# Making layer 1's coefficients in one run ahead of the second aggregation instead of between its steps

## The chip, the cores and the metric

The kernel runs on one core of a Trainium2 chip. What counts is the device time of one execution, in microseconds. Three runs are shown for the kernel before; the time is their median. The profiled execution is a separate one.

## What is computed

Four graph layers follow one another on 1250 nodes with 512 features and 21250 edges, sorted by their target node. The part that matters here is layer 0, which is two relational convolutions, and the coefficients of layer 1:

```python
def _rel_graph_conv(h, src, dst, etypes, norm, basis, comp, bias, loop_w, apply_relu):
    hb = jnp.einsum('nd,bdo->bno', h, basis)
    coef = comp[etypes]
    m = coef[:, 0, None] * hb[0][src]
    for b in range(1, basis.shape[0]):
        m = m + coef[:, b, None] * hb[b][src]
    m = m * norm[:, None]
    agg = jax.ops.segment_sum(m, dst, num_segments=n)
    out = agg + bias + h @ loop_w
...
# layer 1: 32 relations, 8 bases
weight = jnp.einsum('rb,bio->rio', w_comp, bases)
h_rel = jnp.einsum('ni,rio->rno', x, weight)
msg = h_rel[etype, src] * norm
out = jax.ops.segment_sum(msg, dst, num_segments=n_nodes)
```

Layer 0 is called twice with its own weights; its relu'd first result is `h` of the second. Each layer's result is added to its input and normalized.

## The kernel before

**Order of the work.** The program is laid out by hand: each stage writes its instructions for all five engines, and each engine runs its own list in that order, held back by semaphores. The stages are: `prepare` (tables of the sorted edges and the coefficients of layer 0), the first aggregation L0a, the first transform (with `Hidden` as its epilogue), the second aggregation L0b, the second transform, the aggregation L1 of layer 1, its transform, and then layers 2 and 3.

**An aggregation** (`aggregate`, L769) multiplies gathered rows by selectors. GpSimd gathers 168 tiles of 128 edges' source rows by indirect DMA (L809) into a ring of 16 places (`gathered`); SyncE counts their landings (L838). For each of 208 steps VectorE makes a 128 x 128 selector (L945) out of the edge's place in its window and its coefficient, and TensorE multiplies the selector by the tile (L895), in two passes since both are fp32. ScalarE copies a finished window's sum out (L922) and clears the bank (L913, L927). Banks 0 to 3 of PSUM take the sums. Near the end, and after it, TensorE turns the sums (L858) for the transform. VectorE may be 12 selectors ahead. TensorE and VectorE read small tables of step numbers into registers every four steps (L812).

**The coefficients** (`Coefficients`, L603) are the entries of `comp` by the edge's relation, times the edge's weight. For layer 1 there are 62 groups of 4 steps, in 16 batches of 4 groups (the last has 2). A batch k is made in three moves, and every fourth time a fourth:
- `spread(k)` (L684): TensorE spreads the relations of the steps over the partitions, 4 matmuls of 128 columns in 16 bits, stationary tile `step_pickers`, into bank 4. Layer 1 has this one bank for spreads, so `spread(k)` waits for `compare(k - 1)`.
- `compare(k)` (L693): VectorE compares the bank with the relation's number, 512 elements, into `relation_onehot`.
- `pick(k)` (L703): TensorE picks the rows of `comp_blocks`, 4 fp32 matmuls of 32 columns in two passes each, into bank 5 or 6.
- `weigh(k)` (L722): VectorE multiplies 16 groups by the edges' weights into `coef_L1`. There are 4 of these.

Layer 0's coefficients are made in `prepare`, by `on_pe` and `on_dve` of the same class in a row, in 4 batches, with two banks for spreads and 128 columns per pick. Layer 1's are made inside L0b: `beside_on_pe(s)` and `beside_on_dve(s)` put a spread, a compare, a pick and a weighing after every ninth step. The pickers, a copy of 4096 16-bit elements per partition (L661), are laid by ScalarE at L0b's head (`work.lay(act.copy, laid)`).

**Beside the steps of L0b** also runs `OwnProduct`: 10 tiles of h times the loop weight, 4 slices each, two passes a slice (L1027), each slice after a step.

**The head of L0b.** `ready` is what every engine waits for before it begins: the first transform's last products, the turned tiles of h in `xT` (`hidden.done()`, copies L1232 and L1251) and the stores of h to `hidden_rows` in DRAM (L1196, five of them last). The gathers read `hidden_rows`; nothing else in the aggregation does.

Of the kernel before, what the change touches and what calls it, by code (L numbers as in the profile page):

```python
# [13 lines left out]
P = 128  # L14
# [3 lines left out]
D = 512  # L18
# [145 lines left out]
def prepare(C):  # L164
# [355 lines left out]
        engine.wait_ge(*numbered.now())  # L520
    dve.wait_ge(*taken.now())
    dve.wait_ge(*of0.weighed.now())
    C.tables_made = [taken.now(), of0.weighed.now(), keyed.now()]


# [240 lines left out]
SUM_BANKS = 4  # L766


def aggregate(C, name, path, nb, rows, G, ready, counting=None, beside=()):  # L769

# [7 lines left out]
    space, steps, windows, co = M.at, path.steps, path.windows, C.coef[name]  # L780
    xs = M.new("gathered", [P, RING, D])
    sel = M.new("selector", [P, SELECTORS, P])
    grid = C.iota[:, 0:path.nodes]
    gathered = [C.landed(f"gathered{u}") for u in range(LANDINGS)]
    tiles_landed, multiplied = C.event(f"tiles_landed_{name}"), C.event(f"multiplied_{name}")
# [33 lines left out]
    def on_pool():  # L819
        if counting:  # L820
            for t in range(RING):
                gather(t)
        for token in ready:
            pool.wait_ge(*token)
        if not counting:
            for t in range(RING):
                gather(t)
        for first in range(RING, T, BATCH):
            over = [v & COUNTED for v in table(C.steps_of_tile[path][0:1, first - RING:first - RING + BATCH], POOL, 1, steps)]
            for t in range(first, first + BATCH):  # L830
                pool.wait_ge(multiplied.semaphore.sem, over[t - first])
                pool.sem_inc(*place_free.inc())
                gather(t)
# [50 lines left out]

    def on_pe():
        for token in ready:
            pe.wait_ge(*token)
        tiles, rows_of, sums, counts = batch(0)
        for s in range(steps):
            pe.wait_ge(*selected(s + 1))  # L890
            if counting:
                pe.matmul(counts[s % BATCH], counting.rows[:, s % SELECTORS, :], counting.sources[:, s % SELECTORS, :],  # L892
                          start=False, stop=False, skip_group_check=True)
            pe.wait_ge(tiles_landed.semaphore.sem, tiles[s % BATCH])
            pe.matmul(sums[s % BATCH], sel[:, s % SELECTORS, :], rows_of[s % BATCH], start=False, stop=False,  # L895
                      skip_group_check=True).then_inc(*multiplied.inc())
            if (s + 1) % BATCH == 0 and s + 1 < steps:
                tiles, rows_of, sums, counts = batch((s + 1) // BATCH)
            if turns_after(s) is not None:
                turn(turns_after(s))  # L900
            for work in beside:
                work.beside_on_pe(s)
        for j in late:
            turn(j)
# [45 lines left out]
    def on_dve():  # L950
        for token in ready:
            dve.wait_ge(*token)
        if counting:
            dve.wait_ge(*counting.numbered(1))
        for s in range(steps + AHEAD):
            if s < steps:
                if s % BATCH == 0:
                    begun = [v & COUNTED for v in table(C.window_of_step[path][0:1, s:s + BATCH], DVE, 1, windows)]
                select(s, begun[s % BATCH])
            if s >= AHEAD:  # L960
                for work in beside:
                    work.beside_on_dve(s - AHEAD)
                if turns_after(s - AHEAD) is not None:
                    for k in range(KC):
                        take(turns_after(s - AHEAD) * KC + k, dve)
        for j in late:
            for n in range(j * KC, (j + 1) * KC):
                if taker[n] is dve:
                    take(n, dve)
# [92 lines left out]
def plain_lhs(xT):  # L1062
    return lambda k, js: xT[:, k, js[0] * P:(js[0] + len(js)) * P].rearrange("p (j n) -> p j n", n=P)
# [455 lines left out]
def layers_0_1(C):  # L1519

    nc, A, M = C.nc, C.A, C.M
    pe, act, dve, pool, sp = C.engines
    hidden_rows, x1_rows = C.rows("hidden_rows"), C.rows("x1_rows")
    C.x1_rows = x1_rows
    C.count_rows = nc.dram_tensor("count_rows", (NP, NP), F32, kind="Internal").ap()

    G, after_G, counting = C.G0, C.after_G, C.counting
    tail = (M.end - 4 * (2 * NT * D + 2 * D)) // 64 * 64
    M.at = after_G
    turned = aggregate(C, "L0a", PATH0, 4, A["x"], G, C.tables_made, counting)  # L1530

    M.at = tail
    x = M.new("x", [P, NT, D])
    xT = M.new("xT", [P, KC, NP])
    assert M.at <= M.end
    M.at = tail - 4 * HALF * D
    h = M.new("h", [P, HALF, D])
    M.at = after_G
    products = [(basis_lhs(4, G, b), A["L0_gnn_basis0"][b]) for b in range(4)]
    hidden = Hidden(C, h, xT, hidden_rows)  # L1540
    turn_x = TransposeX(C, x, xT, 4 * KC)
    multiplied = transform(C, products + [(plain_lhs(xT), A["L0_gnn_loop0"])], A["L0_gnn_bias0"], turned, [], hidden, turn_x)
    assert M.at <= tail
    M.at = after_G
    ready = multiplied + hidden.done() + [stored.now() for stored in hidden.stored]
    own = OwnProduct(C, tail, x, xT, A["L0_gnn_loop1"], A["L0_gnn_bias1"], ready)
    turned = aggregate(C, "L0b", PATH0, 4, hidden_rows, G, ready, beside=(C.of_layer1, own))

    products = [(basis_lhs(4, G, b), A["L0_gnn_basis1"][b]) for b in range(4)]
    residual = ResidualNorm(C, lambda j: x[:, j, :], x1_rows)  # L1550
    multiplied = transform(C, products, None, turned, [own.added.now()], residual)

    M.at = C.after_layer1_edges
    G = M.new("G1", [P, PATH1.windows, D])
    keep1 = M.at
    ready = multiplied + [residual.ln.normed.now()] + [s.now() for s in residual.stored]
    turned = aggregate(C, "L1", PATH1, 8, x1_rows, G, ready)

    M.at = C.after_small
    C.x_place = M.at  # L1560
    C.x = x = M.new("x_L2", [P, NT, D])
    C.condT, C.condR = M.new_split("condT", [STACKED, NP])
    C.count = M.new("count_by_src", [P, NT, NP])
    C.keep2 = M.at
    C.rows_place = (M.end - 64 - 4 * (2 * N + 2 * NT * 4 * P)) // 64 * 64
    condition = Conditioning(C)
    assert M.at <= C.keep2
    M.at = C.keep2
    C.W2 = M.new("weights2", [P, 2, KC, D])
    assert M.at <= C.after_layer1_edges + 4 * D * PATH1.windows // 2  # L1570
    M.at = keep1
    C.layer1_norm = residual = ResidualNorm(C, lambda j: x[:, j, :], None, x1_rows)
    products = [(basis_lhs(8, G, b), A["L1_gnn_bases"][b]) for b in range(8)]
    C.layer1_done = transform(C, products, A["L1_gnn_h_bias"], turned, [], residual, other=condition)
    C.conditioned = condition.chain.now()
# [1274 lines left out]
```

## Time and profile before

| | us |
|---|---|
| three runs | 3026.91, 3029.58, 3031.84 |
| median | 3029.58 |
| profiled execution, its own time | 3030.57 |
| profiled execution, its span | 3029.2 |

| engine | busy us | share of the span |
|---|---|---|
| TensorE | 2912.4 | 96% |
| VectorE | 1783.0 | 59% |
| ScalarE | 1201.4 | 40% |
| GpSimd | 1117.0 | 37% |

The span is what the trace covers; 1.4 us of the execution's time lie around it. A time inside the span is told from the span's start. L0b begins near 435 and ends near 694. In the views PE is TensorE, PEld its loading of stationary tiles, DVE is VectorE, ACT is ScalarE, POOL is GpSimd, and SP is SyncE with the queue SPq. An engine's busy time is a sum over its instructions; a matmul's end is modelled, so pieces of one engine may overlap. PEclk is the granted clock of TensorE as a share of 2.4 GHz, so that 0.50 is 1.2 GHz.

### The profile page before, as it was taken

What the parts mean: (1) busy time and instruction counts of PE and PEld (TensorE: products, weight loads), DVE (VectorE), ACT (ScalarE), POOL (GpSimd) and SP (SyncE); (2) the same over time, 40 slices, a digit from 0 to 9 for tenths busy, and PEclk for the clock granted to TensorE, in tenths of its full rate; (3) what the DMA queues carried; (4) which work ended last, traced back from release to release, by engine and by line L of the source; (5) the groups of instructions that cost most, each with busy time, mean ns of one, the idle gap of its engine ahead of it and who ended that gap; (6) DMA issues with size and microseconds to landing.
All of it is one profiled execution on the core that took longest, in us unless ns stands there. A gap on an engine that the chain in (4) does not pass through costs nothing.

```text
span 3029.2 us, 43316 instructions
## 1 busy us (share of the span) xinstructions
PE 2912.4 (96%) x14533; PEld 2175.3 (72%) x14533; DVE 1783.0 (59%) x4790; ACT 1201.4 (40%) x2182; POOL 1117.0 (37%) x930
## 2 busy tenths in 40 slices
PE   6999989999799999999999999999999999999999
PEld 3446764457644568764479988899888998789987
DVE  7774224453433632543667677576775767757677
ACT  1333331113244233421545554355543545435454
POOL 4773337663377533411031134311343113431133
PEclk9999999999899999999999999999999999999999
DMA  4775437652277523232030021300213002130022
GB/s 125 206 206 168 133 105 203 175 171 74 90 206 208 154 77 95 70 110 69 28 115 8 8 70 45 112 8 8 70 45 112 8 8 70 45 112 8 8 70 83
DMA packets 129387, 279.13 MB, mean 92 GB/s; under 512 B 22616, under 2 KB 45464, under 8 KB 128144
## 3 DMA queue, kind: packets, MB, share of 16 engines
q0 software_dynamic: 40320, 132.15, 15.1%
q1 hardware_dynamic: 87408, 141.55, 14.7%
q8 instruction: 123, 2.02, 0.3%
q10 hardware_dynamic: 1440, 2.62, 0.2%
q14 instruction: 96, 0.79, 0.1%
HBM read 227.65 MB, written 27.46 MB: 84 GB/s over the span
## 4 chain that ended last, share of the span: by engine, by line
PE 88%; DVE 8%; ACT 2%; DMA 1%; issue 1%; SPq 0%; POOL 0%; DVEq 0%; ACTq 0%; POOLq 0%
PE banks L895 19%; PE banks L159 17%; PE banks L160 17%; PE banks L161 17%; PE banks L2456 6%; PE banks L2120 3%; PE banks L1769 2%; PE banks L858 2%; PE banks L1027 1%; DMA yT_lo<-yT_new_lo 1%; DVE y_tile L2072 1%; DVE y_tile L2074 1%; PE banks L892 1%; DVE columns L2055 1%; DVE G L869 1%
## 5 line engine op out<-in xcount | busy, mean ns | idle before, releaser
L895 PE MATMUL banks<-gathered,selector 128*128 x1328 | 619.3, 598 | 28.5 <-SPq L838 17.0
L895 PEld LDWEIGHTS banks<-gathered,selector 128*128 128x128 f32 x1328 | 239.2, 192 | 299.2 <-issue 220.7
L2544 ACT CAST probT<-banks 128x512 fp32r<-128x512 f32 (+2 forms) x480 | 212.2, 516 | 263.1 <-PE banks L2456 262.3
L1466 POOL TENSOR_TENSOR weight_parts<-weight_ring,weight_parts 128x512 fp32r<-128x512 f32 x130 | 187.7, 1444 | 300.1 <-ACT weight_parts L1399 300.1
L922 ACT COPY G<-banks 128x512 f32<-128x512 f32 x160 | 93.7, 585 | 509.9 <-PE banks L895 509.9
L2625 DVE CUSTOM_DVE_ANT_0 prob<-banks,count_by_src 128x512 f32<-128x512 f32 (+1 forms) x480 | 258.3, 588 | 59.0 <-PE banks L161 59.0
L2552 DVE TENSOR_TENSOR probT<-banks,probT 128x512 fp32r<-128x512 f32 (+2 forms) x480 | 254.2, 585 | 50.6 <-ACT probT L2544 49.9
L159 PE MATMUL banks<-weight_parts,lhs_parts 128*128 128x512 f32 x680 | 269.1, 396 | 15.0 <-DVE lhs_parts L1410 6.2
L160 PE MATMUL banks<-weight_parts,lhs_parts 128*128 128x512 f32 x680 | 267.4, 393 | 0.0
L161 PE MATMUL banks<-weight_parts,lhs_parts 128*128 128x512 f32 x680 | 267.0, 393 | 0.0
L1425 DVE TENSOR_TENSOR lhs_parts<-G,lhs_parts 128x640 fp32r<-128x640 f32 x122 | 101.4, 833 | 275.7 <-ACT lhs_parts L1397 275.5
L159 PE MATMUL banks<-probT,value_parts_hi 128*128 128x256 f32 (+3 forms) x800 | 234.7, 293 | 0.0
L2578 ACT ACTIVATE prob<-prob,columns 128x1250 f32<-128x1250 f32 x160 | 217.7, 1361 | 41.8 <-DVE columns L2632 41.7
L160 PE MATMUL banks<-probT,value_parts_hi 128*128 128x256 f32 (+3 forms) x800 | 222.2, 278 | 0.0
L161 PE MATMUL banks<-probT,value_parts_lo 128*128 128x256 f32 (+3 forms) x800 | 221.5, 277 | 0.0
L2230 POOL TENSOR_TENSOR lhs_parts<-values_and_heads,lhs_parts 128x512 fp32r<-128x512 f32 x80 | 103.1, 1291 | 312.0 <-ACT lhs_parts L2283 311.7
L2456 PE MATMUL banks<-ident,prob 128*128 128x128 f32 (+1 forms) x1600 | 198.2, 271 | 2.5 <-DVE probT L2552 1.7
L1397 ACT CAST lhs_parts<-G 128x640 fp32r<-128x640 f32 x122 | 88.8, 728 | 271.8 <-PE banks L161 271.2
L809 POOL DMA_INDIRECT gathered<-hidden_rows,src_index x168 | 163.3, 972 | 81.5 <-SPq L838 46.6
L809 POOL DMA_INDIRECT gathered<-x_rows,src_index x168 | 162.9, 970 | 82.1 <-SPq L838 34.4
L809 POOL DMA_INDIRECT gathered<-in_x,src_index x168 | 163.9, 976 | 72.2 <-SPq L838 32.5
L1973 POOL CAST head_weights_hi<-head_weights 128x1024 fp32r<-128x1024 f32 x16 | 16.6, 1039 | 456.6 <-DMA columns<-in_L_gnn_bk 456.6
(300 smaller groups left out, 6814.1 us busy)
## 6 DMA issues: line engine op xcount, KB each, us to landing
weight_ring<-in_L_gnn_basis SPq DMA_DIRECT2D x64, 256.0 KB, 2.7
weight_ring<-in_L_gnn_bases SPq DMA_DIRECT2D x64, 256.0 KB, 2.6
x_L<-x_rows SPq DMA_DIRECT2D x50, 256.0 KB, 4.2
x_rows<-x_L SPq DMA_DIRECT2D x50, 256.0 KB, 5.5
yT_hi<-yT_new_hi SPq DMA_DIRECT2D x4, 2560.0 KB, 10.9
yT_lo<-yT_new_lo SPq DMA_DIRECT2D x4, 2560.0 KB
count_rows<-count SPq DMA_DIRECT2D x10, 640.0 KB, 4.2
count_by_dst<-count_rows SPq DMA_DIRECT2D x10, 640.0 KB, 4.2
```

The lines of the kernel that those rows point to most:

```text
L159: pe.matmul(acc, lhs[0], rhs[0], start=start, stop=False)
L160: pe.matmul(acc, lhs[0], rhs[1], start=False, stop=False)
L161: return pe.matmul(acc, lhs[1], rhs[0], start=False, stop=stop)
L809: pool.indirect_dma_start(xs[:, (t + 1) % RING, :], None, rows, index).then_inc(*gathered[t % LANDINGS].inc())
L895: pe.matmul(sums[s % BATCH], sel[:, s % SELECTORS, :], rows_of[s % BATCH], start=False, stop=False, skip_group_check=True).then_inc(*multi ...
L1466: pool.tensor_tensor(weight_parts[:, n % 2, 1, :], ring[:, n % 4, :], weight_parts[:, n % 2, 0, :].bitcast(F32), ALU.subtract).then_inc(*w ...
L2230: pool.tensor_tensor(lhs_parts[:, j % 2, 1], attnT[:, :, j * P:(j + 1) * P], lhs_parts[:, j % 2, 0].bitcast(F32), ALU.subtract).then_inc(* ...
L2456: ins = pe.transpose(bank[3 + q // 4][0:width, (q % 4) * P:(q % 4) * P + rows], prob[0:rows, t % 2, q * P:q * P + width], C.ident[0:rows, ...
L2544: ins = act.copy(hi, of)
L2552: ins = dve.tensor_tensor(lo, of, hi.bitcast(F32), ALU.subtract)
L2578: act.activation(prob[:, t % 2, :], prob[:, t % 2, :], ACT.Exp, bias=nmax[:, t % 2:t % 2 + 1], scale=scale, accum_out=rsum[:, h % 2, t:t + ...
L2625: dve.tensor_tensor_reduce(out=prob[:, s, c:c + width], in0=bank[n][:, 0:width], in1=count[:, t, c:c + width], scale=1.0, scalar=-2.0 * NE ...
```

## The change

- The coefficients of layer 1 are no longer made beside the steps of L0b. `aggregate` gets an argument `ahead`, and TensorE and VectorE run its whole sequence (`on_pe`, `on_dve`) before their first step.
- VectorE waits for the last weighing before it makes its first selector.
- The head's waits are split: `ready` holds the products and the turned tiles; the stores are `stored`, which GpSimd waits for before its gathers, SyncE before the loads of `OwnProduct`, and TensorE after the coefficients. VectorE and ScalarE no longer wait for the stores.
- The pickers are laid by GpSimd ahead of the first transform, as soon as L0a's last step is over, at an address behind the ring and the selectors that nothing uses until L0b.

```diff
@@ prepare
+    C.kinds_made = taken.now()
@@ aggregate
-def aggregate(C, name, path, nb, rows, G, ready, counting=None, beside=()):
+def aggregate(C, name, path, nb, rows, G, ready, counting=None, beside=(), stored=(), ahead=None):
@@
     sel = M.new("selector", [P, SELECTORS, P])
+    if ahead:
+        assert M.at == ahead.place
+        M.at = ahead.end
@@ on_pool
-        for token in ready:
+        for token in ready + list(stored):
             pool.wait_ge(*token)
@@ on_pe
         for token in ready:
+            pe.wait_ge(*token)
+        if ahead:
+            ahead.on_pe(C.kinds_made)
+        for token in stored:
             pe.wait_ge(*token)
         tiles, rows_of, sums, counts = batch(0)
@@ on_dve
         for token in ready:
             dve.wait_ge(*token)
+        if ahead:
+            ahead.on_dve()
+            dve.wait_ge(*ahead.weighed.now())
@@ layers_0_1
+    coming = C.of_layer1
...
+    M.at = coming.place = after_G + 4 * (RING * D + SELECTORS * P)
+    for token in turned.steps_over:
+        pool.wait_ge(*token)
+    coming.lay(pool.tensor_copy, C.event("pickers_laid"))
+    coming.end = M.at
+    M.at = after_G
     multiplied = transform(C, products + [(plain_lhs(xT), A["L0_gnn_loop0"])], A["L0_gnn_bias0"], turned, [], hidden, turn_x)
-    assert M.at <= tail
+    assert M.at <= coming.place and coming.end <= tail - 4 * HALF * D
     M.at = after_G
-    ready = multiplied + hidden.done() + [stored.now() for stored in hidden.stored]
-    own = OwnProduct(C, tail, x, xT, A["L0_gnn_loop1"], A["L0_gnn_bias1"], ready)
-    turned = aggregate(C, "L0b", PATH0, 4, hidden_rows, G, ready, beside=(C.of_layer1, own))
+    ready = multiplied + hidden.done()
+    stored = [stored.now() for stored in hidden.stored]
+    own = OwnProduct(C, tail, x, xT, A["L0_gnn_loop1"], A["L0_gnn_bias1"], ready + stored)
+    turned = aggregate(C, "L0b", PATH0, 4, hidden_rows, G, ready, beside=(own,), stored=stored, ahead=coming)
```

The class that makes the coefficients is the same in both kernels; these are its parts that the change now calls in a row:

```python
    def on_pe(self, types):
        pe.wait_ge(*types)
        pe.wait_ge(*self.blocked)
        self.spread(0)
        for k in range(len(self.batches)):
            if k + 1 < len(self.batches):
                self.spread(k + 1)
            self.pick(k)

    def on_dve(self):
        for k in range(len(self.batches)):
            self.compare(k)
            if k and self.complete(k - 1) is not None:
                self.weigh(k - 1)
        self.weigh(len(self.batches) - 1)
```

TensorE at the head of L0b, before (L684 is a spread, L895 a step, L812 and L882 the reading of a table; a wait stands in brackets):

```order
L1204 MATMUL banks<-ident_49,h_16350 128x128 x3
L812 TENSOR_LOAD registers_by_step_67 [waits tile1_stored,tile0_stored,tile2_stored,turned_by_dve,tile3_stored,turned_by_act,tile4_stored,half_summed,product]
L882 ISA x4
L894 REGISTER_ALU [waits selected]
L895 MATMUL banks<-gathered_17691,selector_17692 128x512 [waits tiles_landed_L0b]
L684 MATMUL banks<-types_by_step_76,step_pickers_18989 128x128 [waits G_zero_act]
```

TensorE at the same place and at the end of the new run, with the change (L685 is a spread, L704 a pick, L903 a step):

```order
L685 MATMUL banks<-types_by_step_76,step_pickers_16353 128x128 [waits steps_taken,turned_by_dve,relations_numbered,turned_by_act,pickers_laid,half_summed,product]
L685 MATMUL banks<-types_by_step_76,step_pickers_16353 128x128 x3
L685 MATMUL banks<-types_by_step_76,step_pickers_16353 128x128 [waits types_compared]
L685 MATMUL banks<-types_by_step_76,step_pickers_16353 128x128 x3
L704 MATMUL banks<-comp_blocks_87,relation_onehot_80 128x32 [waits types_compared]
...
L704 MATMUL banks<-comp_blocks_87,relation_onehot_80 128x32 [waits types_compared]
L704 MATMUL banks<-comp_blocks_87,relation_onehot_80 128x32
L816 TENSOR_LOAD registers_by_step_67 [waits tile3_stored,tile2_stored,tile4_stored,tile1_stored,tile0_stored]
L886 ISA x4
L902 REGISTER_ALU [waits selected]
L903 MATMUL banks<-gathered_17695,selector_17696 128x512 [waits tiles_landed_L0b]
```

All 16 batches now stand ahead of the first step, and the wait for the stores stands behind them. The same on VectorE, with the change (L694 is a compare, L723 a weighing, L953 a selector):

```order
L1262 COPY xT_16349<-banks 128x4x128 [waits tile_turned] x2
L694 TENSOR_SCALAR relation_onehot_80<-banks,relation_90 128x512 [waits turned_by_dve,turned_by_act,types_spread,half_summed,product]
L694 TENSOR_SCALAR relation_onehot_80<-banks,relation_90 128x512 [waits types_spread]
L694 TENSOR_SCALAR relation_onehot_80<-banks,relation_90 128x512 [waits types_spread,comp_picked] x3
L723 TENSOR_TENSOR coef_L_18_66<-banks,weights_78 128x64x8 [waits comp_picked]
L694 TENSOR_SCALAR relation_onehot_80<-banks,relation_90 128x512 [waits types_spread,comp_picked] x4
...
L694 TENSOR_SCALAR relation_onehot_80<-banks,relation_90 128x256 [waits types_spread,comp_picked]
L723 TENSOR_TENSOR coef_L_18_66<-banks,weights_78 128x56x8 [waits comp_picked]
L816 TENSOR_LOAD window_of_step_58 [waits coefficients]
L952 REGISTER_ALU
L953 SCALAR_TENSOR_TENSOR selector_17696<-iota_60,place_in_window_70,coef_L0b_74 128x128 [waits banks_cleared_L0b]
```

The first selector, which stood right behind the copies of xT and the wait for the stores, now stands behind 16 compares and 4 weighings. On GpSimd the copy of the pickers stands between L0a's last gather and the first transform's first rounding:

```order
L813 DMA gathered_5361<-in_x,src_index_61 128x512 [waits multiplied_L0a,tiles_landed_L0a]
L662 COPY step_pickers_16353<-ident_16bit_79 128x4096 [waits selected,multiplied_L0a]
L1444 CAST weight_parts_16356<-weight_ring_16355 128x512 [waits chunk0_in,selected,multiplied_L0a]
L1446 TENSOR_TENSOR weight_parts_16356<-weight_ring_16355,weight_parts_16356 128x512 [waits G_zero_pool]
```

There it stood in ScalarE's list before, at L0b's head.

## Rows read from the trace of the kernel before

**Rows 1.** The page's part 4, the chain that ended last, by engine.
```profile
PE 88%; DVE 8%; ACT 2%; DMA 1%; issue 1%; SPq 0%; POOL 0%; DVEq 0%; ACTq 0%; POOLq 0%
```

**Rows 2.** Stretches: length, PE busy (instructions), PEclk, DMA share, GB/s.
```profile
20.00:25.00 5.00, 5.00 (x23) 1.00 0.31 84
40.00:45.00 5.00, 5.00 (x16) 0.50 0.53 154
430.00:435.00 5.00, 4.07 (x26) 1.00 0.28 102
435.00:440.00 5.00, 0.00 (x0) 0.69 0.44 166
445.00:450.00 5.00, 3.72 (x8) 0.50 0.90 316
450.00:455.00 5.00, 5.00 (x12) 0.94 0.71 206
```

**Rows 3.** Timeline at L0b's head: start, length, instruction, idle before and releaser.
```profile
434.89 0.58 ACT L1232 COPY xT<-banks 128x512 f32<-128x512 f32 x1 [0.48 <-PE banks L1204]
438.90 3.60 ACT L661 COPY step_pickers<-ident_16bit 128x4096 bf16<-128x4096 bf16 x1 [3.42 <-DMA hidden_rows<-h]
439.58 0.98 POOL L809 DMA_INDIRECT gathered<-hidden_rows,src_index  x1 [13.49 <-DMA hidden_rows<-h]
...
448.15 0.63 PE L684 MATMUL banks<-types_by_step,step_pickers 128*128 128x128 bf16 x4
448.83 0.75 DVE L693 TENSOR_SCALAR relation_onehot<-banks,relation 128x512 f32<-128x512 f32 x1
```

**Rows 4.** Chain of waits in order of time, L0b: start, length, piece.
```profile
446.28 2.08 PE banks L895 x2
448.36 0.42 PE banks L684 x4
448.79 4.43 PE banks L895 x8
...
459.22 1.72 PE banks L895 x4
461.16 3.49 PE banks L895 x8
464.65 0.81 PE banks L703 x8
...
629.00 24.11 PE banks L895 x56
...
691.14 2.58 PE banks L895 x6
```

**Rows 5.** Instructions on the tile `gathered` in 430 to 760: ns min/median/max, first and last start.
```profile
L895 PE MATMUL banks<-gathered,selector x416: 592/592/1222, 446.3 to 693.1; 128*128 x139
```

**Rows 6.** Timeline of `prepare`, layer 0's coefficients among it.
```profile
22.84 0.98 PE L504 MATMUL banks<-tile_of_step_onehot,dst_parts 128*128 128x208 bf16 x4
29.01 2.07 PE L703 MATMUL banks<-comp_blocks,relation_onehot 128*128 128x128 f32 x8 [0.42 <-DVE relation_onehot L693]
41.65 1.12 PE L504 MATMUL banks<-tile_of_step_onehot,dst_parts 128*128 128x248 bf16 x4
46.08 0.26 DVE L943 TENSOR_SCALAR onehot_row<-low_numbers_16bit,row_in_window 128x128 bf16<-128x128 f16 x1 [0.45 <-issue]
```

**Rows 7.** Weighings of layer 1 (line L722): ns min/median/max, first and last start.
```profile
L722 DVE TENSOR_TENSOR coef_L<-banks,weights x4: 982/1103/1106, 499.1 to 629.0; 128x512 f32<-128x512 f32 x3, 128x448 f32<-128x448 f32 x1
```

**Rows 8.** Timeline: GpSimd and TensorE at the first transform's start, GpSimd's last gather of L0b.
```profile
259.51 0.61 POOL L1433 CAST weight_parts<-weight_ring 128x512 fp32r<-128x512 f32 x1 [13.62 <-DMA weight_ring<-in_L_gnn_basis]
262.12 1.28 POOL L1435 TENSOR_TENSOR weight_parts<-weight_ring,weight_parts 128x512 fp32r<-128x512 f32 x1
277.37 0.50 PE L159 MATMUL banks<-weight_parts,lhs_parts 128*128 128x512 f32 x1 [1.93 <-DVE lhs_parts L1410]
...
669.89 0.96 POOL L809 DMA_INDIRECT gathered<-hidden_rows,src_index  x1 [0.30 <-SPq L838]
```

## The prediction

> **What bounds the kernel now.** The chain of waits first: TensorE carries 88% of it, so a change counts where it moves TensorE's own work or lets it stand idle [rows 1]. Then the granted clock around the start of the second aggregation (L0b) [rows 2]: TensorE does nothing in 435 to 440, its clock falls from 1.00 to 0.50 (from 2.4 to 1.2 GHz), and it is back only in the stretch from 450. Then the timeline there [rows 3]: the last tile of xT is copied by 435.47, the stores of the hidden rows let the first gather go at 439.58, and the pickers keep ScalarE busy for 3.60. Last the chain inside L0b [rows 4]: the first step begins at 446.28, when its gathered tile has landed, and from there to 693.7 TensorE waits for nothing. So L0b costs an idle head and then a TensorE-bound stream, and the change moves work from the stream into the head. Does what leaves the stream outweigh by how much the first step comes later?
>
> **What leaves the stream.** Fifteen of the 16 batches of layer 1's coefficients are a spread of four 16-bit matmuls and a pick of eight passes; the last is half a batch. Their cost, read from the stream: from 446.28 to 629.00 are 182.7 us. A pass of a step costs 24.11 / 56 = 0.4305 us. Of the 416 passes of L0b [rows 5] 118 come after 629.00 (56, seven groups of eight, six), so 298 lie before: 128.3 us. The ten own products with 4 slices of 2 passes cost 80 x 0.4305 = 34.4. That leaves 20.0 us. The low clock at the start takes 2.4 of them: 2.08 for two passes where 0.86 is the price, 4.43 for eight where it is 3.44, 0.42 for the first spread where 0.22 is. **17.6 us** are left for the batches, 1.1 each: a pick of 0.81 [rows 4], a spread of 0.22 (460.94 to 461.16), and some 0.1 of change-over [rows 4].
>
> **When the first step now begins.** PE, DVE and ACT no longer wait for the stores, so the first spread can go at 435.6 (435.47 and a semaphore) [rows 3]. Only one bank takes spreads, so spread k+1 waits for compare k, and a batch is bound either by that loop or by TensorE's own work on a spread and a pick.
> - The loop: a spread's results are there for the compare 0.68 after its first matmul (448.15 to 448.83, at 1.2 GHz), the compare takes 0.75 [rows 3], a semaphore 0.05: 1.48.
> - TensorE's work depends on the clock. At 2.4 GHz it is 0.22 + 0.81 = 1.03. At 1.2 GHz the spread is 0.42 [rows 4]; no row shows this pick at 1.2 GHz. From below it is 0.81 (nothing doubles), from above the 2.07 of layer 0's pick, which has the same stationary tiles and four times the columns [rows 6]. I take 1.62, twice the high-clock price, since a pass of a step, too, takes at least twice its 0.43 there (2.08 for two) [rows 4]. A batch is then 2.04, TensorE-bound.
>
> Which clock? Layer 0's coefficients in the first 35 us are the same loop, denser. Their row says 1.00, but the durations are those of 1.2 GHz: four matmuls of 208 columns take 0.98 at 22.84, four of 248 take 1.12 at 41.65, where the row says 0.50, the same rate per column [rows 2, 6]. So that work, on an engine busy 5.00 of 5.00, did not lift the clock. And in L0b the clock is high at 435 and falls soon after the gap begins [rows 2]; the new chain starts 0.7 us into that gap. I take one or two batches at 2.4 GHz and the rest at 1.2.
>
> Sum: 15.5 batches x 2.04 = 31.6, so the picks end at 467.2. Then 0.2 until the last is read, 0.98 for the last weighing [rows 7], 0.45 for DVE's register load (its gap before 46.08) [rows 6], 0.35 for the first selector and 0.05: 469.2. The high-clock batches at the beginning give back 0.9 (1.28 each instead of 2.04, and part of the second): 468.3. The first step moves from 446.28 to 468.3, **+22.0**. The steps start at 1.2 GHz as before, so the 2.4 stay. Sum: +22.0 - 17.6 = **+4.4 us**.
>
> **What costs nothing, and under what cover.** The pickers on GpSimd: 4,096 elements a partition are 4.9 us at the 0.61 of its 512-element cast, and at the 1.28 of its two-input pass 10.2; I take 4.9, the nearer kind. A gain is not possible, as nobody waited there. They start when L0a's last step is done, 256.7, and GpSimd's first rounding moves from 259.51 to 266.9 at worst. Its first two chunks, done at 263.40 before, are then done at 270.8, and TensorE asks for the first at 277.37 [rows 8]. Without DVE's and ACT's turning of G there the 10.2 would show. The three weighings inside the chain (1.10 each [rows 7]) delay a compare by some 0.5, inside the 0.56 by which the loop is shorter than TensorE's batch; at 2.4 GHz they show, 0.57 each. ScalarE's 3.60 at 438.90 are freed, but the first step waited for the tile. SP issues what it did, on the same stores. The gathers: the first 16 go as before, from 439.58, fill the ring and wait for the first step; the other 152 cost 1.26 each or less than the stream's pace. Before, the last was issued at 669.89, 21 us ahead of the last steps at 691.14 [rows 4, 8]; that lead is set by the ring and stays, so no step comes to wait for a tile. DVE's compares and weighings leave the steps; TensorE did not wait for them.
>
> The sum against the profiled execution's own 3030.57 is 3035.0; that execution is 1.0 above the median of three, so against 3029.58 it is **3034.0**. A difference under 0.2% (6.1 us) can't be told from none here, and this is 0.15%.
>
> **The rivals.**
> - **The clock stays at 2.4 GHz (15%).** For it: the head's gap is only 0.7 us, and in each batch TensorE is used for 1.03 of 1.28 us. Against: the rows of layer 0. A batch is then the loop, 0.48 + 0.75 + 0.05 = 1.28 (a spread's matmuls 0.20 shorter): 15 are 19.2, the half one 1.3, the delays 1.7, the end 2.0, so the first step is at 459.8, +13.5. The steps start at 2.4 GHz: -2.4. Sum -6.5: 3023.1. The Trainium skill (TensorE: Matmul & The Clock Gate, "HAM oscillation — how this bites in real kernels") warns of gaps between bursts in which TensorE does nothing; read as the only thing that lowers the clock, it would give this rival. The row of 435 to 440 agrees that such a gap lowers it, and layer 0's rows speak against its being the only one [rows 2, 6].
> - **A mixed clock (10%)**, high for half of the batches: 3028 to 3032.
> - **The pick costs layer 0's whole 2.07 (12%)**: at 1.2 GHz its passes are bound by loading 128 x 128 fp32 tiles and don't get under one another, and the next spread waits for their end. A batch is 2.49, 15.5 of them 38.6, the first step at 476.2: +29.9 - 17.6 = +12.3, 3041.9, slower. It decides from a batch of 2.15 us on. For it: a measured row of the same stationary tiles. Against: 0.57 of those 2.07 are the last pass running out, and four times the columns.
> - **The pickers are late or in the way (3%)**: only if the copy took over 16 us; then each us more is one lost at 277.
>
> **How the numbers follow.** The forecast has 60%, its own range 3032 to 3036.5 (batches of 1.95 to 2.15, one to three of them at 2.4 GHz). The range of 8 in 10 reaches from below the high-clock case to the 2.07 case: 3022 to 3042. Faster by over 0.2% is most of the high-clock case: 0.11. Slower by over 0.2% is the 2.07 case, the pickers, and the edge of the forecast's: 0.21. Within: 0.68.
>
> **What would show it.** The first L685 at 435.6 instead of 448.15; sixteen of them 2.0 apart (1.3: first rival; 2.5: third); PEclk 0.50 over most of 437 to 470; the first step near 468; from there to its end a stream of 230, 17.6 shorter, with nothing between steps but own products and turns; GpSimd's copy of 4 to 10 us at 256.7, TensorE's first L159 still near 277. I am wrong in the main point if the clock stays at 1.00 there, or if a batch is not TensorE-bound.

## The result and the profile after

The changed kernel takes 3035.6 us (median of 17 runs, 3029.34 to 3040.04), the kernel before in the same comparison 3029.64 (17 runs). The ratio is 1.0019, with an interval of 1.0012 to 1.0026: 6.0 us longer, inside the 0.2% that was taken as no difference, though above zero. A second comparison of the same two kernels gave 3035.08 against 3030.79, ratio 1.0013 (1.0004 to 1.0022), 4.3 us. The forecast was 3034.0, or +4.4.

The chain of waits of the changed kernel at L0b's head (start, length, piece; lines after 520 have moved, so L685 is the spread, L694 the compare, L704 the pick, L723 the weighing, L903 the step) answers to [rows 3, 4]:

```profile
437.45 0.59 ACT xT L1243
438.05 0.20 issue
438.24 0.40 PE banks L685 x4
438.67 0.05 DVEq L693
438.76 0.76 DVE relation_onehot L694
439.57 0.40 PE banks L685 x4
439.97 0.87 PE banks L704 x8
440.84 0.39 PE banks L685 x4
...
444.04 0.43 PE banks L685 x4
444.47 1.66 PE banks L704 x8
446.12 0.42 PE banks L685 x4
446.55 1.65 PE banks L704 x8
448.20 0.43 PE banks L685 x4
...
467.13 2.52 PE banks L704 x12
469.68 0.99 DVE coef_L L723
470.69 0.34 DVEq L816
471.16 0.36 DVE selector L953
471.52 0.12 issue
471.64 3.78 PE banks L903 x4
```

From the fourth batch on the chain lies on TensorE alone: 0.43 for a spread, 1.65 for a pick, 2.08 from spread to spread. Its end is the short tail of weighing, register load and selector.

The stretches of 5 us (busy time and count of PE, PEld, DVE, ACT and POOL, then PEclk, DMA share, GB/s) give the clock, beside [rows 2]:

```profile
435.00:440.00 5.00, 3.23 (x30) 2.62 (x30) 3.08 (x5) 3.71 (x8) 0.00 (x0) 1.00 0.59 213
440.00:445.00 5.00, 4.95 (x40) 4.75 (x39) 2.67 (x4) 0.34 (x1) 1.96 (x3) 0.76 0.48 164
445.00:450.00 5.00, 5.00 (x30) 5.00 (x30) 2.74 (x4) 0.00 (x0) 3.82 (x4) 0.50 0.98 361
450.00:455.00 5.00, 5.00 (x32) 5.00 (x32) 2.02 (x3) 0.00 (x0) 3.83 (x4) 0.50 0.76 232
```

The clock is at 2.4 GHz for the first batches and then at 1.2 GHz, with TensorE and its loading of stationary tiles (PEld) each busy 5.00 of 5.00.

The instructions on `gathered` in L0b answer to [rows 5], and the timeline of GpSimd at the first transform to [rows 8]:

```profile
L903 PE MATMUL banks<-gathered,selector x416: 592/592/1218, 471.6 to 700.7; 128*128 x139
L813 POOL DMA_INDIRECT gathered<-hidden_rows,src_index x168: 951/957/1102, 442.4 to 678.2; - x168
```
```profile
257.62 3.59 POOL L662 COPY step_pickers<-ident_16bit 128x4096 bf16<-128x4096 bf16 x1 [10.87 <-PE banks L903]
261.17 0.60 POOL L1444 CAST weight_parts<-weight_ring 128x512 fp32r<-128x512 f32 x1
261.85 1.28 POOL L1446 TENSOR_TENSOR weight_parts<-weight_ring,weight_parts 128x512 fp32r<-128x512 f32 x1
```

The pickers put the first rounding back from 259.51 to 261.17, and the last gather is still issued 22 us ahead of the last pass at 700.7 (23 before, 669.89 to 693.1).

**Where the time went.** The two traces don't line up at L0b. The last xT copy starts at 437.45, 2.56 later than before [rows 3], and it can be placed. In L0a TensorE's clock rose a few steps later (0.66 in 50 to 55, before 0.88), so L0a ended 0.9 later; nothing of the change lies there. And in the first transform the clock was down for a few us (0.79 in 280 to 285, before 1.00). Both profiles of the changed kernel have this second fall, but two kernels below that lay the pickers in the same place have not, so it isn't counted as the change's. So everything is measured from that copy, to the start of the last six passes of L0b in the timeline. That timeline ends so in both kernels (before first, then changed):

```profile
690.98 2.74 PE L895 MATMUL banks<-gathered,selector 128*128 x6
```
```profile
698.52 2.74 PE L903 MATMUL banks<-gathered,selector 128*128 x6
```

| kernel (all in the same condition of the chip) | last xT copy | to the first step | first step to last group | both | against before |
|---|---|---|---|---|---|
| before | 434.89 | 11.39 | 244.70 | 256.09 | |
| changed | 437.45 | 34.19 | 226.88 | 261.07 | +4.98 |
| changed, second comparison | 438.40 | 34.40 | 226.66 | 261.06 | +4.97 |
| between the steps, other two parts kept | 435.88 | 11.61 | 244.66 | 256.27 | +0.18 |
| changed, 16-bit picks | 438.88 | 26.26 | 227.45 | 253.71 | -2.38 |
| eight batches ahead, 16-bit picks | 435.10 | 14.07 | 230.56 | 244.63 | -11.46 |

The first step came 22.8 later and the stream was 17.8 shorter: +5.0. The spans differ by 5.1 (3034.3 and 3029.2), because 2.4 of the 2.56 are given back behind L0b. One place shows it: before, TensorE's clock was 0.69 right after L0b, where the changed kernel has 1.00. The stretch from 700 of before and the one from 705 of the changed kernel:

```profile
700.00:705.00 5.00, 5.00 (x17) 3.88 (x17) 1.79 (x2) 0.22 (x1) 1.14 (x1) 0.69 0.29 99
```
```profile
705.00:710.00 5.00, 3.10 (x14) 2.57 (x15) 4.30 (x5) 0.38 (x1) 3.61 (x3) 1.00 0.39 109
```

### The profile page after: what moved, and what is told of

Its sections match the earlier page's. It is cut to its first block, busy times and chain, and to the rows that moved or that the text cites. A ratio compares the mean times of both kernels' runs of the same rounds, so it can differ in the third digit from the quotient of the medians.

```text
span 3034.3 us, 43314 instructions
## 1 busy us (share of the span) xinstructions
PE 2924.8 (96%) x14533; PEld 2188.3 (72%) x14533; DVE 1784.7 (59%) x4790; ACT 1197.8 (39%) x2181; POOL 1121.0 (37%) x931
## 4 chain that ended last, share of the span: by engine, by line
PE 87%; DVE 8%; DMA 2%; ACT 2%; issue 1%; POOL 0%; SPq 0%; DVEq 0%; ACTq 0%; POOLq 0%
PE banks L903 19%; PE banks L159 17%; PE banks L160 16%; PE banks L161 16%; PE banks L2475 6%; PE banks L2139 3%; PE banks L1788 2%; PE banks L862 2%; PE banks L1038 1%; DMA yT_lo<-yT_new_lo 1%; DVE y_tile L2091 1%; DVE y_tile L2093 1%; PE banks L900 1%; DVE columns L2074 1%; PE banks L704 1%; DVE x_L L2306 1%
## 5 line engine op out<-in xcount | busy, mean ns | idle before, releaser
L903 PE MATMUL banks<-gathered,selector 128*128 x1328 | 615.6, 598 | 19.5 <-SPq L842 17.5
L903 PEld LDWEIGHTS banks<-gathered,selector 128*128 128x128 f32 x1328 | 242.1, 192 | 301.8 <-issue 233.2
```

## The experiments

Twelve runs of nine kernels stand below, in three groups. The first and the second ran on one chip, the third on another. In the first and the third the kernel before took 3127.62 and 3128.95 us, against 3030.79 in the second. Each kernel is therefore compared with before in its own group, and traces are compared across groups only for the head and the spacing of batches. The times that were expected in us (3035 to 3036 and the like) were all meant for the condition of 3030.

### First group, with before at 3128: is the batch bound by TensorE, and does filler hold the clock?

**Two banks for the spreads.**
```diff
-    C.of_layer1 = Coefficients(C, PATH1, 32, [(C.coef["L1"], "L1_gnn_w_comp")], (4,), (5, 6), *shared)
+    C.of_layer1 = Coefficients(C, PATH1, 32, [(C.coef["L1"], "L1_gnn_w_comp")], (4, 7), (5, 6), *shared)
```


> The changed kernel with a second bank for layer 1's spreads, so that a spread no longer waits for the compare just before it. Theory (the run ahead is bound by TensorE's own work at 1.2 GHz, 2.08 us a batch): no change, 3035 to 3036, batches still 2.08 apart once the clock is low; only the first three or four batches, at 2.4 GHz, may be 0.2 shorter each. Rival (the loop spread, compare, spread is what bounds a batch): batches fall to 1.1 to 1.5 and the time by 9 to 15 us, to 3021 to 3027.

Measured: 3148.15 against 3127.62, ratio 1.0062 (1.0036 to 1.0087). TensorE's timeline of this kernel:

```profile
481.79 1.03 PE L704 MATMUL banks<-comp_blocks,relation_onehot 128*128 128x32 f32 x8
482.66 0.39 PE L685 MATMUL banks<-types_by_step,step_pickers 128*128 128x128 bf16 x4
482.88 1.07 PE L704 MATMUL banks<-comp_blocks,relation_onehot 128*128 128x32 f32 x8
...
485.71 0.61 PE L685 MATMUL banks<-types_by_step,step_pickers 128*128 128x128 bf16 x4
486.11 1.86 PE L704 MATMUL banks<-comp_blocks,relation_onehot 128*128 128x32 f32 x8
487.79 0.61 PE L685 MATMUL banks<-types_by_step,step_pickers 128*128 128x128 bf16 x4
488.19 1.86 PE L704 MATMUL banks<-comp_blocks,relation_onehot 128*128 128x32 f32 x8
```

At 1.2 GHz batches stay 2.08 apart (485.71 to 487.79); at 2.4 GHz they are 1.09 (481.57 to 482.66) where one bank gave 1.27. So the bank binds only at the high clock, and TensorE binds at the low one. The time can't be set against the changed kernel, which was not run beside it, and the 20.5 us above before have something else in them: VectorE did nothing for 11.89 us in the middle of the run ahead, which no trace of the second group shows. The head is 45.0 (34.2 in the changed kernel), and the stream behind it is longer too, 248.3 (226.9):

```profile
505.66 0.75 DVE L694 TENSOR_SCALAR relation_onehot<-banks,relation 128x512 f32<-128x512 f32 x1 [11.89 <-remote]
```

**One filler matmul, and four, behind each pick.**
```diff
             self.pick(k)
+            if self.relations == 32:
+                for _ in range(1):
+                    pe.matmul(self.C.bank[7][:], self.C.ident16[:],
+                              self.pickers[:, 0:4, :].rearrange("p g r -> p (g r)"), start=True, stop=True)
```
(`range(4)` in the other.) Their results are not used.

> The changed kernel with one more 16-bit matmul of 512 columns behind each pick, whose result nobody reads. Theory (the clock falls because the run uses TensorE too sparsely): if one filler holds the clock at 2.4 GHz, a batch is 1.28 to 1.35, the first step comes 9 to 10 us earlier and starts at full clock, 3023 to 3026. If it doesn't, a batch is 2.08 + 0.43 = 2.5 and the time 3041 to 3043. Rival (the clock in the run costs nothing, a batch is bound by VectorE): 3035 to 3036 either way.

> The same with four fillers behind each pick: TensorE is nearly always streaming. Theory: the clock stays at 2.4 GHz; a batch is 0.22 + 0.81 + 4 x 0.215 = 1.9, so the first step comes at about the changed kernel's own time or 2.5 us earlier, and the steps start at full clock, which saves 2.5 to 3 more: 3030 to 3034. If the clock falls all the same, a batch is 2.08 + 4 x 0.43 = 3.8 and the time 3061 to 3065. The batch length and the granted clock of the run tell it apart.

Measured: 3152.67, ratio 1.0086 (1.0067 to 1.0104), with one; 3162.74, ratio 1.0122 (1.0101 to 1.0143), with four. That is 25 and 35 us above before, where 3023 to 3043 was expected with one, and 3030 to 3034 or 3061 to 3065 with four; and each trace has an idle time of VectorE in the run ahead (10.59 and 13.99), so only the batches are read. With one filler the clock fell after two batches, and the batch was 2.51 (480.24 to 482.75). With four, in this trace, it did not fall:

```profile
480.00:485.00 5.00, 5.00 (x42) 3.58 (x42) 1.65 (x3) 0.00 (x0) 2.92 (x3) 1.00 0.63 190
485.00:490.00 5.00, 4.54 (x40) 3.34 (x38) 2.61 (x3) 0.00 (x0) 3.83 (x4) 1.00 0.98 352
490.00:495.00 5.00, 1.50 (x10) 0.76 (x9) 0.00 (x0) 0.00 (x0) 3.84 (x4) 0.98 0.71 211
```

Batches were 1.95 apart up to an idle time of 13.99 of VectorE at 489.3; after it they ran at 1.2 GHz, 3.79 each, to the end of the run ahead, with TensorE busy 5.00 of 5.00 from 505 to 540. The first half looked like proof that fillers hold the clock. The second half and the repeat below took it back.

**Five batches ahead, eleven between the steps.**
```diff
-    PACE = 9
+    PACE, AHEAD = 9, 5
...
     def beside_on_pe(self, s):
         k, at = divmod(s, self.PACE)
+        k += self.AHEAD
...
-            ahead.on_pe(C.kinds_made)
+            ahead.ahead_on_pe(C.kinds_made)
```


> The changed kernel with only the first five of the 16 batches ahead of the first step, the other eleven after every ninth step as before. Theory (a batch ahead is free as long as it lies in the 10.7 us in which the first gathered tile is still on its way, and costs 2.08 after that, while it saves 1.1 in the stream): five batches end near 445.6 on the clock of before, the first step stays within 1 us of its old place, and 5 x 1.1 = 5.6 us leave the stream: 3024 to 3026. Rival (taking them out of the stream saves less than 0.6 each, or the head is longer for another reason than the batches): 3028 to 3034.

Measured: 3129.4, ratio 1.0002 (0.9988 to 1.0015). The first step came 11.52 after the last xT copy (11.39 before), so the five batches did fit into the head. The gain that should have followed is not in the time.

### Second group, with before at 3031: beside the changed kernel itself

> The changed kernel itself, so that the others of this call have it beside them on their own chip. Both theories: if the chip is like that of the first comparison, +4 to +7 us against the kernel before. On the chip of the first four experiments DVE once had nothing to do for 11 to 14 us inside the run ahead (its releaser is shown as another core or an unknown queue); if that comes with the chip and not with my edits, the changed kernel has such a gap there too and stands +10 to +25 us. If it came with the edits alone, +4 to +7 there as well.

Measured: 3035.08 against 3030.79, ratio 1.0013 (1.0004 to 1.0022). No idle time of VectorE of this kind stands in its trace, on the same chip as the first group. That speaks for a condition of the chip and against the edits as the source of the idle times; the two-bank and filler kernels themselves were not run in this condition. The batches are the same: 0.43 and 1.65.

**Before's order, with the other two parts of the change kept.**
```diff
+    coming.lay(pool.tensor_copy, C.event("pickers_laid"))
...
-    turned = aggregate(C, "L0b", PATH0, 4, hidden_rows, G, ready, beside=(C.of_layer1, own))
+    turned = aggregate(C, "L0b", PATH0, 4, hidden_rows, G, ready, beside=(coming, own), stored=stored, ahead=coming)
```


> Before's order (coefficients between the steps of the second aggregation), with the change's other two parts kept: GpSimd lays the pickers at the first transform, and the first gathers no longer wait for the hidden rows' tables. My theory (both parts are hidden, all of the change's time comes from the order): 0 us against the kernel before, +-2. Rival (the pickers on GpSimd or the split wait cost or save time by themselves): off by 3 us or more, and the first step of the second aggregation not at its place of before.

Measured: 3031.02 against 3030.79, ratio 0.9999 (0.999 to 1.0007). The head is 11.61 and the stream 244.66, within 0.3 of before. TensorE waits for the stores before its first step here, as before, so the split wait is kept for VectorE and ScalarE alone. The pickers on GpSimd and this split are worth nothing by themselves; the change's time is all in the order, which is what uses the earlier start.

**The picks in 16 bits.** The entries of `comp_blocks` are kept as a high and a low 16-bit part, so layer 1's coefficients have another precision; two small VectorE instructions in `prepare` make the parts.
```diff
+                onehot = C.onehot[:, k % 2, :].bitcast(BF16)[:, n * P:(n + 1) * P]
+                for half in range(2):
+                    ins = pe.matmul(to, onehot, self.blocks16[:, half, :], start=half == 0, stop=half == 1)
```


> The change, with layer 1's picks as two bfloat16 matmuls (the coefficients kept as a high and a low 16-bit part, so their precision is different) in place of one float32 matmul each. My theory (the run ahead is bound by TensorE, 0.42 for the spread and 1.66 for the pick of 2.08 us a batch): the pick falls to 0.86 at 1.2 GHz or less, the batch to 1.3 to 1.5 us, where the loop spread, compare, spread binds; the first step comes 9 to 10 us earlier, so -7 to -11 us against the change and 0 to -5 against the kernel before. Rival A (the batch is held by DVE and the hand-over between the engines): the batch stays at 1.9 or more, within 3 us of the change. Rival B (a float32 pick is not longer than two bfloat16 ones): the same as rival A, with the pick itself at 1.5 or more in the trace.

Measured: 3028.09, ratio 0.9987 (0.9979 to 0.9996) to before, 7.0 us under the changed kernel. TensorE's timeline and one stretch:

```profile
446.41 0.61 PE L694 MATMUL banks<-types_by_step,step_pickers 128*128 128x128 bf16 x4 [0.70 <-DVE relation_onehot L706]
446.81 0.42 PE L720 MATMUL banks<-comp_blocks_16bit,relation_onehot 128*128 128x32 bf16 x8
447.97 0.61 PE L694 MATMUL banks<-types_by_step,step_pickers 128*128 128x128 bf16 x4 [0.75 <-DVE relation_onehot L706]
```
```profile
445.00:450.00 5.00, 2.84 (x42) 2.53 (x42) 3.07 (x4) 0.00 (x0) 3.82 (x4) 0.50 0.99 349
```

The eight matmuls of a pick take 0.42 where the fp32 ones take 1.86 in this view. TensorE now waits 0.7 for each compare, and the batch is mostly 1.53 at 1.2 GHz: the loop through one bank, which the prediction had at 1.48. The compare takes 0.75 as before, though it writes 16 bits. The head is 8.1 shorter than the second profile of the change (26.26, 34.40), where 9 to 10 were expected, and 15.5 batches at 0.55 less each make 8.5 of it. With the second bank's 2.08, this shows that the price of the fp32 pick at the low clock set the changed kernel's head.

**Eight batches ahead, eight between, with the 16-bit picks.** The methods that split the run are those of the five batches.
```diff
-    PACE = 9
+    PACE, AHEAD = 9, 8
```


> Eight of the sixteen batches ahead of the first step, the other eight between the steps as before, with the bfloat16 picks. My theory (before, the tensor engine waits some 11 us for the first gathered rows, and work laid into that wait is free while each batch between steps costs 1.1 us): eight batches of 1.3 us take 10.4 us and fit, so the first step stays within 1 us of its place of before, and the stream is shorter by 8 x 1.1 = 9 us, with the remaining picks a little shorter: -8 to -12 us against the kernel before, -14 to -18 against the change. Rival (the gap is already used, or a cold clock at its end takes the gain back): -3 to +3 against before.

Measured: 3021.63, ratio 0.9968 (0.9955 to 0.9981): 9.2 us under before, 13.4 under the changed kernel. It beats both. The head is 14.07, 2.7 over before, where at most 1 was expected. The batches are the loop's 1.53 at 1.2 GHz, and the last pick starts at 447.42. The timeline names a selector as what the first step waited for; but the first selector was made by 447.62 and the first tile was counted as landed at 446.77. What lies between the last pick and the step is TensorE's own reading of its step table: in the trace its load starts at 447.65 and takes 0.85, four register instructions follow, and the step starts at 449.17 (timeline, the loads of that table in 440 to 452, and the chain further on):

```profile
449.17 2.07 PE L940 MATMUL banks<-gathered,selector 128*128 x2 [1.36 <-DVE selector L991]
L853 PEldq TENSOR_LOAD <-registers_by_step x2: 847/848/849, 447.6 to 449.7; - x2
```
```profile
467.29 0.19 PE banks L720 x8
```

Where the gain is from can be reckoned. A pick between the steps now costs 0.19 where it cost 0.81 [rows 4], 0.62 less. Eight batches gone at 1.1 are 8.8, the other 7.5 have cheaper picks, 4.7, and the head takes 2.7 back: 10.8, and the trace has 11.46 (its run was 6.6 under the median of the five). By the same prices the cheap picks alone, in before's order, would give 15.5 x 0.62 = 9.6. That kernel was not run, so it is reckoned and not shown that the place of the eight batches gives only some 1 to 2 us.

### Third group, on another chip, with before at 3129: the first questions again

> The change with two banks for the spread types in place of one, a second time: in its first call all kernels and the kernel before ran some 100 us longer, with idle times of DVE of 11 to 15 us that a second run of the change did not show. My theory (TensorE binds the batches): batches stay 2.08 us apart at 1.2 GHz, the time within 1 us of the change, +3 to +7 against the kernel before. Rival (the hand-over through the one bank binds): batches at 1.3 to 1.7 and -6 us or more against the change.

Measured: 3155.09 against 3128.95, ratio 1.0075 (1.0057 to 1.0094). Batches are 2.08 apart again, and VectorE has an idle time of 10.50 in the run ahead again; the head is 45.8 and the stream 249.0. The spacing is as expected for TensorE; the time is not (+3 to +7).

> The change with four matmuls of 512 columns (some 0.86 us, into an unused bank) behind each pick of the run ahead, a second time. Theory A (dense column work holds TensorE at 2.4 GHz, sparse picks of 32 columns do not): the granted clock stays at 1.00 through the run ahead, the batch is 0.21 + 0.87 + 0.86 = 1.95 us, and the steps of the aggregation start at 0.43 each: -2 to -6 us against the change. Theory B (the clock falls in the run ahead whatever the matmuls are): the batch is 0.43 + 1.66 + 1.72 = 3.8 us, +25 us or more against the change.

Measured: 3172.21, ratio 1.014 (1.0118 to 1.0161). The same kernel as in the first group, and the other outcome: the clock was down before the first pick and stayed down to the end of the run, with TensorE busy 5.00 of 5.00 in 480 to 495 (it then sat idle for 7.22).

```profile
475.00:480.00 5.00, 4.05 (x20) 2.85 (x19) 1.50 (x2) 1.81 (x4) 0.99 (x1) 0.61 0.28 79
480.00:485.00 5.00, 5.00 (x25) 3.90 (x24) 1.43 (x2) 0.00 (x0) 3.83 (x4) 0.50 0.97 343
485.00:490.00 5.00, 5.00 (x23) 3.62 (x23) 0.82 (x2) 0.00 (x0) 3.82 (x4) 0.50 0.87 282
```

A batch is then 3.78. The two profiles of one kernel show both levels, so filler of this size decides nothing: theory A fell as a rule, and theory B too, since the first trace is against it. What picks the level is open.

> Five of the sixteen batches ahead, the rest between the steps, picks in float32, a second time. My theory (the wait of 11 us before the first step takes in the five batches, 3 x 1.25 + 2 x 2.08 = 7.9 us and a weighing): the first step within 1 us of its place of before, five batches fewer between the steps at 1.1 us each: -4 to -6.5 us against the kernel before, -8 to -12 against the change. Rival (the batches ahead delay the first step by what they save): -2 to +2 against before.

Measured: 3132.06, ratio 1.0006 (0.9993 to 1.0018). The head is 11.44, as expected; the time is not shorter. A miss, twice. Behind the head this trace has idle times of this group's kind, on ScalarE and VectorE, and TensorE's clock falls with one of them (510 to 515 and after):

```profile
ACT G L951 <- remote: 18.2, 1, 18.2
DVE x L1068 <- remote: 15.0, 1, 15.0
```

The kernel before was not profiled in this condition, so where the expected 4 to 6.5 went stays open. That five fp32 batches ahead save time was never measured.

**Eight batches ahead, 16-bit picks, two banks in the run ahead.**
```diff
+    def spread_bank(self, k):
+        if self.relations == 32 and k < self.AHEAD:
+            return (4, 7)[k % 2]
+        return self.spread_banks[k % len(self.spread_banks)]
```


> The eight batches ahead with bfloat16 picks, now with two banks for the spread types in the run ahead. In the eight batches with one bank they were 1.53 us apart at 1.2 GHz, held by the loop spread, compare, spread, with TensorE busy less than 60%, and the first step came 2.7 us later than before. My theory: with two banks the batch falls to 1.0 to 1.2 us, the first step comes 2 to 3 us earlier, where the first gathered rows bind again: -2 to -3 us against one bank, -10 to -13 against the kernel before. Rival (the gathered rows bind already): 0 +-1 against one bank.

Measured: 3127.66 against 3128.95, ratio 0.9997 (0.9984 to 1.001). The head is 11.36, 2.7 shorter than with one bank and at before's 11.39, as expected. But the second bank isn't shown to be the reason, since the clock differs too: it stayed high for most of the batches here, and fell after the third spread with one bank. The spreads were about 0.75 apart, less than expected; VectorE made six compares in a row in 4.44, so at this clock it is the compare that binds:

```profile
475.00:480.00 5.00, 3.32 (x67) 2.50 (x67) 3.95 (x6) 2.24 (x5) 0.77 (x1) 1.00 0.34 122
480.00:485.00 5.00, 1.62 (x34) 1.06 (x30) 3.88 (x12) 0.00 (x0) 3.78 (x5) 0.80 0.97 324
```

The time missed what was expected (-10 to -13), in the condition in which the five batches missed theirs, too; an idle time of 10.72 of VectorE between two weighings stands in its stream. Whether it would beat 3021.63 beside a before of 3031 was not tried.

## Why the prediction was right

- **What leaves the stream.** 17.6 was forecast and 17.8 measured. The low clock at its first steps cost more: the first ten passes took 7.05 where 4.31 is the price, 2.75 and not 2.4. With that apart the batches were worth 18.2. The kernel with before's order has a stream of 244.66, so nothing else in the change touches it.
- **The batch.** Forecast 2.04, TensorE-bound; measured 2.08, and bound as said: a second bank left it at 2.08, a cheaper pick brought it to the loop. The pick that no row had shown at 1.2 GHz was taken at 1.62 and is 1.65. The rival with 2.07 was to decide from a batch of 2.15 on; in the view of its row the new pick takes 1.86, from spread to spread it adds 1.65. The reason given against this rival, four times the columns, was no reason: in the trace of before, layer 0's passes of 128 columns start 0.21 apart at 1.2 GHz, and the new ones of 32 columns do too (1.65 / 8). With PEld busy 5.00 of 5.00 this speaks for the loading of the tiles as the price, as that rival had it, though its passes do get under one another.
- **The clock.** Forecast one or two batches at 2.4 GHz; measured two at 1.27 and 1.29, a third of 1.91, then 0.50 to the end. The rival of a high clock is out for the changed kernel, in both its profiles, and none of its 28 runs is under 3029.34, where that rival had 3023.1.
- **The head.** Forecast +22.0; measured +22.8, mostly 15.5 times the 0.04 of the batch. The tail behind the last pick was 1.99 where 2.0 was worked out.
- **What costs nothing.** Both parts, shown by the kernel that keeps them with before's order: 0.2 us in L0b. GpSimd's copy took 3.59 and not 4.9; TensorE's first product of the transform is at 278.23 after 277.37, the 0.9 by which L0a ended later.
- **The sum.** +4.4 forecast, +5.0 in L0b, 5.1 between the spans, 6.0 and 4.3 between medians.

What was not foreseen is the disorder around it: the clock's rise and fall in places that the change doesn't touch moved the profile by 2.6 one way and 2.4 back. The prediction says that less than 6.1 us can't be told apart in one comparison; with 17 and 11 runs both intervals lie just above 1, and both traces place 5.0 in L0b, so the loss is real, if small.

The Trainium skill (TensorE: Matmul & The Clock Gate, "HAM oscillation — how this bites in real kernels"), read as gaps being all that lowers the clock, was the prediction's first rival. The changed kernel has gaps of 0.83 and 0.95 us before its first two spreads in the run ahead, after which TensorE was busy 4.95 of 5.00 while the clock fell, and 5.00 of 5.00 over the 20 us from 445 to 465, in which it stayed at 0.50. The first profile with four fillers has the same two gaps and kept 1.00. Idle gaps as the only cause don't account for that, so the traces are against this reading.

## What to carry to other kernels

Work moved off a TensorE-bound stream into a gap is paid at the gap's price: here 1.1 us a batch between the steps became 2.08 in a row, at half the clock. Only what fits into the wait that stands there anyway (11.4 us here) leaves the first step where it was, as five batches and eight cheap ones with two banks did; what is over puts the whole stream off by its own length. A gain in the time itself was measured for one such kernel alone, the eight cheap batches. And before moving a costly piece, make it cheap, if its precision allows: 16-bit picks took 1.86 to 0.42 at the low clock, and by these prices, reckoned and not run, that is worth more here than any place for them.

## What the runs showed of the hardware

- GpSimd copied 4096 16-bit elements a partition in 3.59 us, ScalarE in 3.60 [rows 3], though GpSimd's cast of 512 fp32 elements takes 0.61 [rows 8], which is a third more per element.
- Two profiles of one kernel, the four fillers, had TensorE at 2.4 and at 1.2 GHz over the same batches, 1.95 or 3.78 us each. One of them had both levels, before and after an idle time.
- Eight fp32 passes of 32 columns with a 128 x 128 stationary tile take 1.65 at 1.2 GHz and 0.87 at 2.4 GHz in the chain, nearly twice as long at half the clock, and at 1.2 GHz passes of 128 columns start no further apart (0.21); eight 16-bit matmuls of the same shape take 0.19 in the chain at 2.4 GHz.
- One chip had the kernel before at 3128 us in the first group and at 3031 in the second; another had it at 3129 in the third. In the traces of the first and the third VectorE or ScalarE sat idle for 7 to 25 us at a time with the releaser shown as another core or an unknown queue (`remote` in the rows), or as none, all before 1120 us, while DMA packets (within one) and bytes are the same. Some of the places recur: in the two-bank kernel VectorE's idle times end at 506, 660 and 699 on one chip and at 504, 665 and 700 on the other, with five batches ahead at 513 and 514. The cause is open. Where such a time falls into a run ahead that lies on the chain, the first step comes later by about as much: with two banks and 16 batches ahead the heads were 45.0 and 45.8 against 34.2, with 11.9 and 10.5 of idle time in them.
